# A mixture-of-experts router fed with rows ahead of their layer norm: weights centred once, logits scaled by each row's inverse deviation

## The reference, cut to what matters

```python
x = x + jnp.tanh(g_xattn[0]) * _L0_xattn_ref(_layernorm(x, axis=-1), ctx_2048, ...)      # x1
x = x + jnp.tanh(g_ffn[0]) * _L0_ffn_ref(_layernorm(x, axis=-1), gate_weight, ...)       # h = layernorm(x1)
# inside _L0_ffn_ref, with x = h (2048 rows of 512) and gate_weight (8, 512):
router_logits = x @ gate_weight.T
probs = jax.nn.softmax(router_logits, axis=-1)
top_v, top_i = jax.lax.top_k(probs, 2)
top_v = top_v / top_v.sum(axis=-1, keepdims=True)
# every expert: hidden = silu(h @ gate.T) * (h @ up.T);  y = hidden @ down.T;  out += weight * y
```

## Time and profile before

| what | value |
|---|---|
| time, median of 3 runs | 939.45 us (938.52 to 940.46) |
| time of the profiled execution | 937.56 us |
| its span, first to last instruction | 935.8 us |
| TensorE busy (PE) | 902.2 us, 96% |
| VectorE (DVE), ScalarE (ACT), GpSimd (POOL) busy | 433.5, 384.1, 269.6 us |
| mean granted TensorE clock | 0.979 |

### The profile page before, as it was taken

How to read it: one execution, slowest core, us unless ns; L and a number is a source line. 1 busy time by engine, 2 the same in 40 slices (tenths; PEclk the granted TensorE clock), 3 DMA queues, 4 the chain that set the end, 5 groups by cost and what they waited for, 6 DMA issues and landing times.

```text
span 935.8 us, 14697 instructions
## 1 busy us (share of the span) xinstructions
PE 902.2 (96%) x4327; PEld 729.7 (78%) x4328; DVE 433.5 (46%) x805; ACT 384.1 (41%) x743; POOL 269.6 (29%) x332
## 2 busy tenths in 40 slices
PE   8998999999799999999999999999999999999994
PEld 7766877789578888888888888888888888888883
DVE  7888787695932114513613616321721272136111
ACT  5676767435222224424423526222622352244221
POOL 6428484751511211311221222112212121112211
PEclk9999999995799999999999999999999999999998
DMA  8220502038351123622622715412631272211121
GB/s 299 74 85 12 169 28 106 23 138 292 108 209 23 34 34 101 217 43 64 251 36 37 283 37 184 142 23 38 214 107 34 34 260 54 44 23 23 34 34 23
DMA packets 27843, 92.90 MB, mean 99 GB/s; under 512 B 5104, under 2 KB 5104, under 8 KB 21296
## 3 DMA queue, kind: packets, MB, share of 16 engines
q1 hardware_dynamic: 19008, 72.03, 20.9%
q0 software_dynamic: 8672, 20.62, 12.0%
q10 hardware_dynamic: 144, 0.02, 0.0%
HBM read 73.98 MB, written 18.68 MB: 99 GB/s over the span
## 4 chain that ended last, share of the span: by engine, by line
PE 89%; DVE 4%; ACT 3%; issue 2%; DMA 1%; DVEq 0%; POOL 0%; ACTq 0%; POOLq 0%
PE bank L264 76%; PE bank L1625 3%; PE bank L1611 2%; PE bank L1431 2%; PE bank L1309 1%; PE bank L1367 1%; PE bank L1425 1%; PE bank L1347 1%; PE bank L1317 0%; DVE sc L481 0%; ACT ex L1067 0%; DMA c_raw<-in_ctx_t 0%; DMA xg<-h_rows,slot_idx 0%; DVE rden L422 0%; DVE tok_tile L706 0%
## 5 line engine op out<-in xcount | busy, mean ns | idle before, releaser
L264 PE MATMUL bank<-g_hi,gt_hi 128*128 128x512 f32 x592 | 236.6, 400 | 0.9 <-DVE gt_lo L732 0.9
L264 PE MATMUL bank<-g_hi,gt_lo 128*128 128x512 f32 x592 | 233.6, 395 | 0.0
L264 PE MATMUL bank<-g_lo,gt_hi 128*128 128x512 f32 x592 | 233.4, 394 | 0.0
L762 DVE TENSOR_TENSOR hid<-silu,bank 128x256 f32<-128x256 f32 x148 | 61.3, 419 | 307.0 <-ACT silu L1274 307.0
L1274 ACT ACTIVATE silu<-bank 128x256 f32<-128x256 f32 x148 | 56.7, 383 | 252.9 <-PE bank L264 237.2
L978 POOL COPY g_idx<-slot_idx 128x1 int32 x37 | 6.9, 186 | 469.8 <-ACT w_nxt L1288 469.8
L264 PEld LDWEIGHTS bank<-g_hi,gt_lo 128*128 128x128 f32 x592 | 110.9, 187 | 27.2
L264 PEld LDWEIGHTS bank<-g_hi,gt_hi 128*128 128x128 f32 x592 | 110.9, 187 | 26.6 <-issue 1.1
L264 PEld LDWEIGHTS bank<-g_lo,gt_hi 128*128 128x128 f32 x592 | 111.0, 187 | 25.6
L264 PE MATMUL bank<-dn_hi,hd_hi 128*128 128x512 f32 x296 | 126.0, 426 | 0.0
L264 PE MATMUL bank<-dn_hi,hd_lo 128*128 128x512 f32 x296 | 117.0, 395 | 0.0
(11 more groups left out here) (238 smaller groups left out, 1293.6 us busy)
## 6 DMA issues: line engine op xcount, KB each, us to landing
raw<-in_w_exp SPq DMA_DIRECT2D x48, 1024.0 KB, 5.4
xs<-in_x SPq DMA_DIRECT2D x4, 1024.0 KB, 7.2
out_rows<-xr SPq DMA_DIRECT2D x16, 256.0 KB, 2.1
h_rows<-dh SPq DMA_DIRECT2D x16, 256.0 KB, 2.1
xr<-in_x SPq DMA_DIRECT2D x3, 1024.0 KB, 5.5
raw<-in_w_attn SPq DMA_DIRECT2D x8, 256.0 KB, 6.2
raw<-in_w_attn SPq DMA_DIRECT2D x2, 1024.0 KB, 13.6
rows<-in_b_rows SPq DMA_DIRECT2D x1, 1024.0 KB, 14.0
```

The source lines that it names most:

```text
L264: mm = eng.matmul(psum, a(k), b(k), start=(first and k == 0 and j == 0), stop=(last and k == n - 1 and j == 2))
L762: dve.tensor_tensor(hid[:, p, :], silu[:, p, :], bank[p][:, 256:512], ALU.mult).then_inc(hid_done, 1)
```

## The change

The router no longer multiplies h but x1.

- The router weights are centred once, near the start: GpSimd fills a 128 x 128 block of `ht` with 1/512, TensorE multiplies it with the weights (their mean over the 512 rows, on every partition), VectorE subtracts that from `gate_w`.
- `h_transposes` transposes `xr` (x1) and waits for `x1_done` instead of `h_done`.
- `keep_logits` multiplies by `rsh` and waits for `hrstd`.
- h itself is still written and stored, for the experts' gather. In batch 3, ScalarE writes it behind the transpose's copy and no longer ahead of it.
- Since `xr` is read by TensorE now, its reload and the next writes of it wait for `h_tr`, and GpSimd's overwriting of `rsh` in batch 3 waits for batch 2's logits.
- On TensorE, the transposes and router products of batch 2's tiles move one place ahead among `last_o_product`, one group of six filler transposes goes, and the first transposes of batch 3 follow.

```diff
@@ start: vector, gpsimd, tensor
+            dve.wait_ge(gate_mm, 1)
+            dve.tensor_tensor(gate_w, gate_w, bank[2][:, 0:E].unsqueeze(1).to_broadcast([P, KC, E]),
+                              ALU.subtract).then_inc(gate_centred, 1)
             for k in range(KC):
                 x_low(0, k, True)
...
+            pool.memset(ht[:, 0, 0, :], 1.0 / H).then_inc(gate_ones, 1)
...
             pe.wait_ge(kv_sb, 2)
+            pe.wait_ge(gate_ones, 1)
+            pe.wait_ge(cload, 16)
+            for k in range(KC):
+                mm = pe.matmul(bank[2][:, 0:E], ht[:, 0, 0, :], gate_w[:, k, :], start=(k == 0), stop=(k == KC - 1))
+            mm.then_inc(gate_mm, 1)
             first_x_transposes()
@@ sync, batch(b, back)
-                if not back:
+                if back:
+                    sp.wait_ge(h_tr, b * TT)
+                else:
                     sp.wait_ge(kv_mm, 1 + NB)
                 sp.dma_start(xr[:, :, :], x_b[b]).then_inc(rload, 16)
@@ vector, update_and_residual and keep_logits
                     if last:
                         dve.wait_ge(last_xb, r + 1)
                         dve.wait_ge(x1_store[r], 16 * NB)
+                        dve.wait_ge(h_tr, (n - 1) * TT + r + 1)
...
                     dve.wait_ge(h_store[u], (n + 1) * 16)
-                    if last:
-                        dve.wait_ge(h_tr, (n - 1) * TT + u + 1)
...
+                dve.wait_ge(hrstd, n * TT + t + 1)
+                dve.tensor_scalar(logits[...], h_bank(t, True)[:, 0:E], rsh[:, t:t + 1], None, ALU.mult).then_inc(lg_done, 1)
@@ gpsimd, tail of the last batch
                 if t >= 1:
+                    pool.wait_ge(lg_done, LAST * TT + t)
                     inverse_h(LAST, t - 1)
@@ scalar, keep_logits and the tail
+                act.wait_ge(hrstd, n * TT + t + 1)
                 act.activation(logits[...],
-                               h_bank(t, False)[:, 0:E], ACT.Copy).then_inc(lg_done, 1)
+                               h_bank(t, False)[:, 0:E], ACT.Copy, scale=rsh[:, t:t + 1]).then_inc(lg_done, 1)
...
-            normalise_h(NB - 1, 0)
             for t in range(TT):
                 h_copy(NB - 1, t, tail=True)
-                if t < TT - 1:
-                    normalise_h(NB - 1, t + 1)
+                normalise_h(NB - 1, t)
             act.wait_ge(d_mm, NT)
@@ tensor, h_transposes and the tail
-                pe.wait_ge(h_done, n * TT + t + 1)
-                if t >= 2 and not tail:
+                pe.wait_ge(x1_done, n * TT + t + 1)
+                if t >= 2 and not tail or t < 2 and tail:
                     pe.wait_ge(lg_done, n * TT + TT + t - 1)
                 for k in range(KC):
-                    tr = pe.transpose(h_bank(t, tail)[:, k * P:(k + 1) * P], dh[:, t, k * P:(k + 1) * P], ident[:, :])
+                    tr = pe.transpose(h_bank(t, tail)[:, k * P:(k + 1) * P], xr[:, t, k * P:(k + 1) * P], ident[:, :])
...
             last_o_product(0)
+            h_transposes(LAST - 1, 1)
             last_o_product(1)
-            h_transposes(LAST - 1, 1)
-            last_o_product(2)
             router(LAST - 1, 1)
             h_transposes(LAST - 1, 2)
-            last_o_product(3)
+            last_o_product(2)
             router(LAST - 1, 2)
             h_transposes(LAST - 1, 3)
+            last_o_product(3)
+            router(LAST - 1, 3)
             pe.wait_ge(dgam, LAST * TT + 1)
-            stay_busy(6, tail_bank[0])
-            router(LAST - 1, 3)
             for t in range(TT):
                 h_transposes(NB - 1, t, tail=True)
```

More of the change, by code:

```diff
@@ L244, in flamingo_gated_block @@
         pad_store = sem("pad_rows_stored")
+        gate_ones, gate_mm, gate_centred = (sem(n) for n in ("gate_mean_selector", "gate_mean_product", "gate_centred"))
         entry, entry_tok = sem("slot_entries_placed"), sem("slot_entries_token")
@@ L473, in keep_logits @@
                 dve.wait_ge(lg_mm, n * TT + t + 1)
-                dve.tensor_copy(logits[:, bass.ds(n * TT + t, 1), :].rearrange("p a e -> p (a e)"),
-                                h_bank(t, True)[:, 0:E]).then_inc(lg_done, 1)
+                dve.wait_ge(hrstd, n * TT + t + 1)
+                dve.tensor_scalar(logits[:, bass.ds(n * TT + t, 1), :].rearrange("p a e -> p (a e)"),
+                                  h_bank(t, True)[:, 0:E], rsh[:, t:t + 1], None, ALU.mult).then_inc(lg_done, 1)
             def clip(b, s, first=False):
@@ L1208, in _ @@
             keep_logits(LAST - 1, 0)
+            h_copy(LAST - 1, 1)
             normalise_h(LAST - 1, 1)
-            h_copy(LAST - 1, 1)
-            normalise_h(LAST - 1, 2)
             keep_logits(LAST - 1, 1)
             h_copy(LAST - 1, 2)
+            normalise_h(LAST - 1, 2)
+            h_copy(LAST - 1, 3)
+            keep_logits(LAST - 1, 2)
             normalise_h(LAST - 1, 3)
-            keep_logits(LAST - 1, 2)
-            h_copy(LAST - 1, 3)
             keep_logits(LAST - 1, 3)
```

## The result

The changed kernel takes 934.44 us, median of 5 runs (933.33 to 934.71), the kernel before 939.25 (938.00 to 940.46, 5 runs). The ratio is 0.9946 with a 95% interval of 0.9935 to 0.9957: 0.54% less, which the interval puts between 4.0 and 6.1 us; the medians lie 4.8 us apart. The forecast was 934.7. The profiled execution took 934.38 us, its span 932.7, the mean granted clock 0.984.

The account below looks back on a forecast made before the run. The prediction took TensorE, busy 96% of the span, as the bound, with time to gain between attention and the expert loop. Its terms, -5.6 + 0.8 = -4.8 us, took the median 939.45 to 934.7 us; range 932.6 to 938.2.

Parts of the forecast that it names:

- Centring, +0.8: At the start, ahead of the first transposes: four small TensorE products cost 0.8 us, bounds 0 to 0.95.
- In the loop and the reload of `xr`, 0: Batch loop: transposes waiting for x1 gain 0; `xr`'s reload, issued 6 to 7 us later, stays hidden by 8 us.
- End of batch 2, gain 2.0: Passage to batch 3: its first transposes can start at about 208.0 instead of 210.0, gain 2.0 us.
- 208.8: Sign: batch 3's first transposes at about 208.8 (208.0 + 0.8), directly behind the last router product.
- Four tiles, clock full, gain 5.6: Batch 3's tiles at full clock: TensorE's logits 7.4 us earlier, but ScalarE's chain limits the gain to 5.6 us.
- The first reduction: Sign in batch 3's tail: the routing's first reduction comes 6 to 7 us earlier than at 225.40.
- the count's place: Sign in the routing: VectorE waits for ScalarE's exponential where it had waited for TensorE's count.
- It did not fall around a wait of 2.68 us: At 74.32: the clock stayed up around TensorE's 2.68 us wait, with full matmuls on both sides.
- the 932.8 for the profiled execution: Forecast for the profiled execution: from 937.56 to 932.8 us, with a span of 931.0.
- the clock falls as before: Rival, batch 3's tiles: half clock from 209.8 on, gain 3.1 - 0.8 = 2.3 us, so 937.1; chance 0.20.
- The rival of the late weights: Rival, tail: expert weights arrive too late for ScalarE's splits; slower, 942.6 with the queue twice as crowded; chance 0.05.
- The clock comes back too late: Rival, start of expert loop: clock rises too late, losing 1.6 us; net gain 3.2, so 936.2; chance 0.10.

Follow-up runs that it names:

- The old order: Kernel after with TensorE's former order at the end of batch 2 (transposes and router products one place later, six fillers back): 936.57 us, ratio 0.9969.
- with the store moved: Kernel after with TensorE's former order at the end of batch 2 and the combine weights' store issued by GpSimd: 933.98 us, ratio 0.9945.
- the second of the kernel before: Profile from the rerun of the kernel before, no edit: median 939.36 us, ratio 1.000; the profiled execution took 939.4 us.
- two variants: Kernel after without the filler groups in batch 3's four tiles, 934.53 us; kernel after with TensorE's former order and GpSimd issuing the `cw` store, 933.98 us.
- the second profile of the kernel after: Profile from the rerun of the kernel after, unchanged: median 934.39 us, ratio 0.9951 against the kernel before.
- the early exponential: Kernel after with ScalarE's exponential ahead of the third weight split instead of behind it: 933.27 us, ratio 0.9942.

## Why the prediction was right, and where it was not

- **Centring, +0.8: right.** +0.79 at the first query product, and it could be hidden in the wait behind it, which the prediction took for part of the same chain and not for room.
- **In the loop and the reload of `xr`, 0: as forecast.** The balance above closes without a term for either, and the reload can be read off: it went out at 161.37, needed 5.1 us to land and was first used at 179.01, so it had 12.5 us of room. Neither was varied by itself.
- **End of batch 2, gain 2.0: right in place, but not for its reason alone.** The tiles begin directly behind the router product, as forecast; 210.48 is 208.8, the 1.5 us from 76 us and 0.2 more. But these 2 us are not what the tail is worth: once the clock stays up, VectorE's x1 every 3.37 us is the path, and the start of the first tile has room. The old order shows it in its rows (ScalarE's h no later behind `nmh`) and, with the store moved, in its time. What the order does secure is the early store of batch 2's last h. And alone it gains nothing in the median.
- **Four tiles, clock full, gain 5.6: right, 5.3 to 5.9 by the pairs of profiles above.** The clock was 1.00 until 219.5, past the 213 that was claimed. The last tile started with its x1, and the exponential took the count's place as what VectorE waits for. Its time is `nmh` 219.41 + 0.27, then h and three splits, 225.89: 6.2 us behind the end of `nmh`, where the forecast had 0.80 + 5.50 + 0.1 = 6.4. The first reduction came 4.74 us earlier in the first two traces; between profiles that agree about 76 us it came 6.5 (225.40 to 218.88, both without the stretch) and 6.1 us earlier (226.77 to 220.66, both with it), against 6 to 7.
- **"It did not fall around a wait of 2.68 us": the sentence that failed.** It was read from one execution. In eleven of the twelve profiles with that wait, the two of the kernel after and the second of the kernel before among them, the clock was half behind it. It cost some 1.5 us on both sides, so the forecast against the median held, while the 932.8 for the profiled execution was 1.6 too low, and a gain of 1.5 us that filling the wait gives was not seen.
- **The rival "the clock falls as before"** was rightly kept. It is not what the two profiles of the kernel after show, but single executions of two variants do, 2 and 4 us dear. Why the clock stays up in one execution and falls in another of the same kernel stays open, so that part of the forecast had a chance and not a reason. **The rival of the late weights** had the right queue and the wrong victim: not ScalarE waiting for weights, but a small store behind them (in the old order ScalarE did wait 0.94 us for its fourth piece, but behind the exponential). It did not decide here by 1.1 us in one profile and by next to nothing in the other; in the old order it did.
- **The clock comes back too late**: hardly. It rose at 243.4, 4.1 us ahead of the first product, against 3.4 before. In the second profile of the kernel after it rose at 245.8, 1.9 us ahead of it, and the product came 6.3 us behind the gather instead of 5.9: 0.4 us, where the rival had 1.6.

On the price of a low clock, first the rows: the kernel before has 3.4, 20.5 and 10.2 us at half clock (second profile: at 75 us, in the tail and ahead of the experts), the kernel after 3.5 in the tail, 13.4 ahead of the experts and about 3.4 at 76 us, 13.8 us less in all, and the change without its start's 0.8 is worth 5.6. Filling 3.4 us of it at 76 us gave 1.46. The Trainium skill, page "TensorE: Matmul & The Clock Gate", section Terms, puts the penalty at the throttled time times (1 - K/N). By it an estimate is 6.9 for the one and 1.7 for the other. The trace agrees where TensorE paces the work, at 76 us, and less so in the tail, where VectorE and then ScalarE take over.

## What to carry to other kernels

Follow a moved chain through every in-order queue it passes, the DMA queue too: here ScalarE's splits set the size of the gain, and a 64 KB store that was issued behind a wait and two 1 MB loads was at least half of the 2 us that an order of instructions cost. A wait of TensorE that no one can shorten may still be worth filling, since the clock behind it can cost more than the filler; and one profile does not tell whether the clock falls, so compare its time with the median before its rows are taken as typical. Look whether two edits gain only together: x1 as the source made the order possible, and the order kept the queue free. When a chain has been shortened, look again at what had been nearly late before: the same store ate a third of the gain of the early exponential.

## What the runs showed of the hardware that was not expected

- Behind the same wait of TensorE, 2.68 to 2.73 us at 75 us, the granted clock stayed full in one profiled execution, was 0.5 for 3.4 us in eight and for 6.8 us in three. With 0.94 and 0.95 us of idle time in its place it stayed full in both profiles.
- Transposes and router products that left TensorE no idle time (17.10 us busy of 17.10) ran at 0.50 all the while in one execution of the old order with the moved store, and like ones at 1.00 in the kernel after. A busy engine in the records is no sign of a full clock.
- A store of 256 KB, 2.1 us to landing by the median of all stores of h, took 11.63 us when 1 MB weight loads were under way. The `cw` store of 64 KB took 8.0 to 8.8 us with two such loads issued just ahead of it, 3.0 to 3.8 us in the kernel before (issued 5 us or more behind them), and from GpSimd 7.8 us when such loads followed 0.8 us behind it and 4.1 us when they followed 3 us behind. Another queue did not make it land much quicker beside the loads; it let it leave sooner.
